# A state-space block with FFN on one core: the scan inside the chunks as a tree, in 13 steps

## The reference, cut to what matters

```python
s = sigmoid(silu(x @ s_w1.T + s_b1) @ s_w2.T + s_b2)
u = (x @ B_w.T + B_b) * s
def step(h, u_t):
    h = h @ A.T + u_t
    return (h, h)
_, hs = jax.lax.scan(step, h0, swapaxes(u, 0, 1))
y = hs @ C_w + C_b + x @ D_w.T + D_b
attn = y * sigmoid(x @ g_w.T + g_b)
x = x + layernorm(attn of layernorm(x))
x = x + layernorm(ffn of layernorm(x))      # square(relu(xf @ Ws1)) @ Ws2 + routed part
```

## Time and profile before

| what | value |
|---|---|
| median of 3 runs | 800.49 us (800.29 to 800.89) |
| the profiled execution | 800.6 us, of which the trace's span is 798.6 |
| PE busy | 783.3 us, 98% of the span |
| DVE, POOL, ACT busy | 605.9, 456.4 and 344.4 us |
| granted clock of PE | 0.998 of full speed |

### The profile page before, as it was taken

The page is one execution under the profiler, slowest core; times in us unless marked ns, Lnnn a source line. Parts: engine busy times, 40 slices in busy tenths (PEclk is TensorE's granted clock), DMA queues, the critical chain, the costliest instruction groups (busy, mean ns, idle before and its releaser), DMA issues. The chain is left out here.

```text
span 798.6 us, 10778 instructions
## 1 busy us (share of the span) xinstructions
PE 783.3 (98%) x3628; PEld 648.0 (81%) x3628; DVE 605.9 (76%) x1404; ACT 344.4 (43%) x554; POOL 456.4 (57%) x553
## 2 busy tenths in 40 slices
PE   7999999999999999999999999999999999999996
PEld 6878888888888888888888888888888888888875
DVE  7868896598956897678975889649896589734895
ACT  4535354344434554245443535435443444432353
POOL 1253658548465576466674665845757557644445
PEclk9999999999999999999999999999999999999999
DMA  8534434454355425552345533454425442232222
GB/s 269 207 107 158 137 94 138 160 184 134 87 177 174 161 89 158 183 187 80 95 143 185 185 101 96 147 185 168 149 80 182 150 143 80 78 133 87 65 113 106
DMA packets 40767, 110.90 MB, mean 139 GB/s; under 512 B 7044, under 2 KB 24836, under 8 KB 32903
## 3 DMA queue, kind: packets, MB, share of 16 engines
q1 hardware_dynamic: 40278, 110.00, 41.4%
q10 hardware_dynamic: 432, 0.20, 0.1%
HBM read 60.84 MB, written 33.61 MB: 118 GB/s over the span
## 5 line engine op out<-in xcount | busy, mean ns | idle before, releaser
L499 PE MATMUL TM<-gw_hi,xT_hi 128*128 128x512 f32 x256 | 107.3, 419 | 0.0
L1982 POOL TENSOR_TENSOR xres<-work,xres 128x512 f32<-128x512 f32 x56 | 75.1, 1341 | 52.8 <-DVE work L1332 52.8
L501 PE MATMUL TM<-gw_hi,xT_lo 128*128 128x512 f32 x256 | 100.6, 393 | 0.0
L501 PE MATMUL TM<-dw_hi,xT_lo 128*128 128x512 f32 x256 | 100.2, 391 | 0.0
L500 PE MATMUL TM<-gw_lo,xT_hi 128*128 128x512 f32 x256 | 100.0, 391 | 0.0
L499 PE MATMUL TM<-dw_hi,xT_hi 128*128 128x512 f32 x256 | 99.9, 390 | 0.0
L500 PE MATMUL TM<-dw_lo,xT_hi 128*128 128x512 f32 x256 | 99.6, 389 | 0.0
L996 ACT ACTIVATE work<-TM,nmz,rsz 128x512 f32<-128x512 f32 x62 | 48.2, 777 | 106.7 <-POOL nmz L1952 106.7
L1942 POOL TENSOR_TENSOR rsv<-rsv,negh 128x1 f32<-128x1 f32 x64 | 47.1, 736 | 82.3 <-DVE rsv L1328 82.2
L1997 POOL TENSOR_TENSOR x2T_lo<-work,x2T_hi 128x512 fp32r<-128x512 f32 x60 | 78.5, 1319 | 2.0 <-ACT x2T_hi L926 1.9
L1990 POOL TENSOR_TENSOR work<-work,xres 128x512 f32<-128x512 f32 x60 | 76.7, 1295 | 1.3 <-ACT work L996 1.3
(11 more groups left out here) (189 smaller groups left out, 2063.1 us busy)
## 6 DMA issues: line engine op xcount, KB each, us to landing
xres<-in_x SPq DMA_DIRECT2D x16, 1024.0 KB, 5.9
x_scratch<-xres SPq DMA_DIRECT2D x16, 1024.0 KB, 4.7
xin<-in_x SPq DMA_DIRECT2D x15, 1024.0 KB, 5.3
work<-x2q SPq DMA_DIRECT2D x120, 128.0 KB, 2.7
out<-work SPq DMA_DIRECT2D x30, 512.0 KB, 3.2
xin<-in_x_t SPq DMA_DIRECT2D x14, 1024.0 KB, 6.2
rows_in<-ln_scratch SPq DMA_DIRECT2D x14, 512.0 KB, 4.7
xin<-in_x SPq DMA_DIRECT2D x2, 512.0 KB, 5.0
```

The costliest lines, as they stand in the source:

```text
L499: eng.matmul(ps, lhs[0], rhs[0], start=first, stop=False)
L501: return eng.matmul(ps, lhs[1], rhs[0], start=False, stop=last)
L1982: eng.tensor_tensor(xres[:, j, :], work[:, j, :], xres[:, j, :], ALU.add).then_inc(S["x1_ok"], 1)
```

## The change

The part of the scan inside the chunks becomes a tree. Up: step 0 adds `A u_0, A u_2, A u_4, A u_6` to `u_1, u_3, u_5, u_7` (one product of 512 columns, one add of 512), step 1 adds `A^2 u_1, A^2 u_5` to `u_3, u_7` (256 columns), step 2 adds `A^4 u_3` to `u_7` and gives `carry`. Steps 3 to 9 are the doubling as before. Down: step 10 adds `A^4 carry` to `u_3`, step 11 adds `A^2` times `carry` and `u_3` to `u_1` and `u_5` (two products of 128), step 12 adds `A` times `carry`, `u_1`, `u_3`, `u_5` to `u_0`, `u_2`, `u_4`, `u_6` (products of 128 and 384 columns, one add of 512). Counted over a batch, 21 products become 15, with 2561 columns in both; 15 adds become 13, with 1793 columns before and 2561 after. The state of position 0 is ready only with step 12, for which `hs` of tile 0 now waits.

Four powers (A^3, A^5, A^6, A^7) are left out: 21 products and copies become 17. The orders of PE, DVE, ACT and POOL in the tails are written anew; in the startup DVE subtracts the first row of "b" earlier, and `low("d")` stands ahead of the second `u_of`. On POOL `z_rs` of tile 4 goes ahead of `ln1_rs`. The diff, cut to its core; DVE's lists of the tails are shown as order below:

```diff
-        POW = [1, 2, 3, 4, 5, 6, 7, 8, 16, 32, 64, 128, 256, 512]
+        POW = [1, 2, 4, 8, 16, 32, 64, 128, 256, 512]
...
-            POWERS += [(at[q], PA, at[q - 1]) for q in {1: (3,), 2: (5, 6, 7)}.get(k, ())]
-            if 3 * k in POW and k >= L:
-                POWERS.append((at[3 * k], plain, at[2 * k]))
...
                 if i == 0:
-                    for j in range(L - 1):
-                        m = eng.matmul(SC[:, 0:P], apt[:, idx[L - 1 - j], :], u[:, j, :],
-                                       start=(j == 0), stop=(j == L - 2))
-                elif i <= 7:
-                    s = 2 ** (i - 1)
+                    m = eng.matmul(SC[:, :], apt[:, idx[1], :], u[:, 0:7:2, :], start=True, stop=True)
+                elif i == 1:
+                    m = eng.matmul(SC[:, 0:2 * P], apt[:, idx[2], :], u[:, 1:6:4, :], start=True, stop=True)
+                elif i == 2:
+                    m = eng.matmul(SC[:, 0:P], apt[:, idx[4], :], u[:, 3, :], start=True, stop=True)
+                elif i <= 9:
+                    s = 2 ** (i - 3)
                     m = eng.matmul(SC[:, s:P], apt[:, idx[L * s], :], carry[:, 1:1 + P - s], start=True, stop=True)
+                elif i == 10:
+                    m = eng.matmul(SC[:, 0:P], apt[:, idx[4], :], carry[:, 0:P], start=True, stop=True)
+                elif i == 11:
+                    eng.matmul(SC[:, 0:P], apt[:, idx[2], :], carry[:, 0:P], start=True, stop=True)
+                    m = eng.matmul(SC[:, P:2 * P], apt[:, idx[2], :], u[:, 3, :], start=True, stop=True)
                 else:
-                    j = i - 8
-                    prev = carry[:, 0:P] if j == 0 else u[:, j - 1, :]
-                    m = eng.matmul(SC[:, 0:P], apt[:, 0, :], prev, start=True, stop=True)
+                    eng.matmul(SC[:, 0:P], apt[:, idx[1], :], carry[:, 0:P], start=True, stop=True)
+                    m = eng.matmul(SC[:, P:4 * P], apt[:, idx[1], :], u[:, 1:6:2, :], start=True, stop=True)
                 m.then_inc(S["scan_done"], 1)
...
                 scan_step(*a, 6)
                 G(*a, 2, {0: 7, 1: 8, 2: 9})
                 scan_step(*a, 10)
-                scan_step(*a, 11)
-                G(*a, 3, {1: 12})
-                scan_step(*a, 13)
-                scan_step(*a, 14)
+                G(*a, 3, {0: 11, 2: 12})
 
             def tail(b, rep):
                 a = (b, rep)
-                G(*a, 0, {0: 0, 1: 1, 2: 2})
+                G(*a, 0, {0: 0, 2: 1})
+                scan_step(*a, 2)
                 W1f(*a, 1, 0)
                 scan_step(*a, 3)
-                W1f(*a, 1, 1, {0: 4})
-                G(*a, 1, {0: 5, 1: 6})
-                scan_step(*a, 7)
-                G(*a, 2, {1: 8, 2: 9})
-                scan_step(*a, 10)
+                W1f(*a, 1, 1, {0: 4, 2: 5})
+                G(*a, 1, {0: 6, 1: 7})
+                scan_step(*a, 8)
+                G(*a, 2, {1: 9, 2: 10})
+                scan_step(*a, 11)
                 W2(*a, 4)
-                scan_step(*a, 11)
+                scan_step(*a, 12)
                 W2(*a, 5)
-                scan_step(*a, 12)
-                G(*a, 3, {2: 13})
+                G(*a, 3)
...
             def last_tail(b, rep):
                 a = (b, rep)
                 G(*a, 0, {2: 0})
-                scan_step(*a, 1)
-                W1f(*a, 1, 0, {1: 2, 2: 3})
-                scan_step(*a, 4)
-                W1f(*a, 1, 1, {0: 5, 1: 6})
-                scan_step(*a, 7)
-                G(*a, 1, {0: 8, 1: 9})
-                G(*a, 2, {1: 10, 2: 11})
+                W1f(*a, 1, 0, {0: 1, 2: 2})
+                scan_step(*a, 3)
+                W1f(*a, 1, 1, {0: 4, 1: 5, 2: 6})
+                G(*a, 1, {0: 7, 1: 8})
+                G(*a, 2, {0: 9, 1: 10})
...
             def hs(b, rep, j):
 
-                if j < L - 1:
-                    eng.wait_ge(S["scan_ok"], body_at("scan_ok", b, 8 + j))
+                if j == 0:
+                    eng.wait_ge(S["scan_ok"], body_at("scan_ok", b, 12))
...
             def scan_add(b, rep, i):
                 eng.wait_ge(S["scan_done"], body_at("scan_done", b, i))
-                if i == 0:
+                if i == 2:
 
                     if rep > 0:
                         eng.wait_ge(S["hs_hi_ok"], body_at("hs_hi_ok", b - 1, L - 1))
                     r = eng.tensor_tensor(carry[:, 1:P + 1], SC[:, 0:P], u[:, L - 1, :], ALU.add)
-                elif i <= 7:
-                    s = 2 ** (i - 1)
+                elif 3 <= i <= 9:
+                    s = 2 ** (i - 3)
                     r = eng.tensor_tensor(carry[:, 1 + s:P + 1], SC[:, s:P], carry[:, 1 + s:P + 1], ALU.add)
+                elif i == 10:
+                    r = eng.tensor_tensor(u[:, 3, :], SC[:, 0:P], u[:, 3, :], ALU.add)
                 else:
-                    j = i - 8
-                    r = eng.tensor_tensor(u[:, j, :], SC[:, 0:P], u[:, j, :], ALU.add)
+                    n, to = {0: (4, slice(1, 8, 2)), 1: (2, slice(3, 8, 4)), 11: (2, slice(1, 6, 4)),
+                             12: (4, slice(0, 7, 2))}[i]
+                    r = eng.tensor_tensor(u[:, to, :], SC[:, 0:n * P].rearrange("p (j n) -> p j n", n=P), u[:, to, :],
+                                          ALU.add)
                 r.then_inc(S["scan_ok"], 1)
...
+            ft_low(-1, -1, 0)
             ln1_norm(0, 1)
-            ft_low(-1, -1, 0)
             less_first_of("s1")
             ln1_norm(0, 2)
             ln1_norm(0, 3)
             l1_bn(0, 4)
+            less_first_of("b")
             l1_bn(0, 5)
...
             ft_low(-1, -1, 3)
-            less_first_of("b")
...
 
             def tail(b):
+                z_rs(b - 1, 4)
                 ln1_rs(b + 1, 0)
-                z_rs(b - 1, 4)
```

More of the change, by code:

```diff
@@ L814, in _ @@
             power(16)
-            power(17)
             H(-1, -1, 0, 0)
@@ L1016, in tail @@
                 zn(*a, 4)
+                hs(*a, 0)
                 zn(*a, 5)
+                gate(*a, 3)
                 hs(*a, 1)
-                gate(*a, 3)
                 zn(*a, 6)
@@ L1474, in first_tail, with tail @@
                 scan_add(*a, 0)
+                scan_add(*a, 1)
+                l1_bn(b + 1, 0)
+                scan_add(*a, 2)
+                l1_ag(b + 1, 0)
+                scan_add(*a, 3)
+                l1_bn(b + 1, 1)
+                scan_add(*a, 4)
+                l1_bn(b + 1, 2)
+                scan_add(*a, 5)
+                scan_add(*a, 6)
+                scan_add(*a, 7)
+                l1_bn(b + 1, 3)
+                scan_add(*a, 8)
+                l1_ag(b + 1, 1)
+                l1_ag(b + 1, 2)
+                l1_ag(b + 1, 3)
+                l1_bn(b + 1, 4)
+                l1_ep(b + 1, 0)
+                l1_bn(b + 1, 5)
+                scan_add(*a, 9)
+                scan_add(*a, 10)
+                scan_add(*a, 11)
+                l1_ag(b + 1, 4)
+                scan_add(*a, 12)
+                l1_ag(b + 1, 5)
+                l1_bn(b + 1, 6)
+                l1_bn(b + 1, 7)
+                l1_ag(b + 1, 6)
+                hs_low(*a, 0)
+                l1_ag(b + 1, 7)
+                hs_low(*a, 1)
+                l1_ep(b + 1, 1)
+            def tail(b, rep):
+                a = (b, rep)
+                scan_add(*a, 0)
                 l1_bn(b + 1, 0)
@@ L1487, in first_tail @@
                 scan_add(*a, 7)
+                l1_ag(b + 1, 2)
+                l1_ag(b + 1, 3)
+                l1_bn(b + 1, 6)
+                h2(*a, 1, 1)
                 scan_add(*a, 8)
                 scan_add(*a, 9)
-                hs_low(*a, 0)
-                l1_ag(b + 1, 2)
-                l1_ag(b + 1, 3)
+                l1_bn(b + 1, 7)
+                scan_add(*a, 10)
+                scan_add(*a, 11)
                 l1_ep(b + 1, 0)
-                scan_add(*a, 10)
-                l1_bn(b + 1, 4)
+                z_bn(*a, 4)
@@ L1861, in _ @@
             h1(-1, -1, 1, 1)
+            low("d")
             u_of(-1, -1, 1)
-            low("d")
             first_tail(0, 0)
```

118 lines of the change are left out of this document (33 added, 85 removed).

## The result

The changed kernel takes 802.91 us (median of 6 runs, 802.00 to 804.33) against 800.39 for the kernel before (800.18 to 800.89): ratio 1.0033, 95% interval 1.0022 to 1.0043. It is slower by 2.5 us, where 0.2 less was forecast, and just outside the range (802.8). Its profiled execution took 802.94 us with a span of 800.8.

What follows compares the result with a forecast made beforehand. PE was taken to bound every stage. Startup +0.4, first tail -0.7, six middle tails +0.1 and last tail -0.1 made -0.3 on the profiled 800.6 us; with the median 0.1 lower, 800.2 us, range 798.2 to 802.8.

Steps and rivals of the forecast that it cites:

- What bounds the kernel, and the price of a scan matmul: Whole kernel: PE bounds every stage; float32 products take two passes at two clocks a column, 0.87 us for 512 columns.
- the rival of one clock a column: All eight tails: a 512-column pass streams at one clock a column, 7.6 us less, 792.6; chance 6%.
- Steps that come too soon: Middle tails: new waits ahead of step 2 and step 9 offset the shorter work; six tails give +0.1 us.
- Step 2's 0.08: Middle tails: PE waits 0.08 us ahead of step 2, three products after the 256-column step 1.
- The 0.04 behind the second h2: Middle tails: add 8 stands behind the second h2 on DVE, so step 9 waits about 0.04 us.
- DVE's queue in the middle tails: Rival, six middle tails: add 8 comes 0.3 to 0.6 us late at step 9, 801.9 to 803.7; chance 18%.
- Startup: Before the first tail: subtraction for b delays the hidden layer, powers left out give 0.5 us back; net +0.4 us.
- The two powers: Startup, behind the first hidden layer: two of four omitted power products leave PE's queue, saving about 0.5 us.
- First tail: Batch 0's tail: two old waits go, step 10 waits 0.65 us and step 2 0.08; net -0.7 us.
- no two steps touch, so 1.3 us goes: First tail: products now stand between all steps, so the two waits at L543 vanish, -1.3 us.
- Last tail: Last batch's tail: h2 stands behind add 9, so no such wait, and less work gives -0.1 us.
- What else moves: POOL's later layernorm statistics, and hs of tile 0 on DVE: both stay hidden from PE, costed at nothing.

Runs made afterwards that it cites:

- e1: One of four follow-up kernels with the changed kernel's DVE startup order, first hidden layer at +0.43 to +0.59; which edit and time carry this label is not told.
- e4, e5, e7: Another of those four follow-up kernels, its startup clock held in the profile; which edit and time carry this label is not told.
- the four together: Changed kernel with DVE's old startup order (low part of d unmoved), first tail's step 12 later and add 9 earlier, last tail's step 1 ahead of FFN products: 801.28 us.

## Why the prediction was wrong

**What bounds the kernel, and the price of a scan matmul: right.** 512 columns cost 0.87, PE's busy time stayed (783.3 to 783.1 us), the first two middle tails fell by 0.10 and 0.04 us, and the rival of one clock a column (792.6) is refuted by every trace. The Trainium skill's four passes for a true float32 product ("FP8 and Floating Point Precision", section "TensorE Precision Notes") agree with the 0.87; its 518 cycles for 512 columns ("TensorE: Matmul & The Clock Gate", section "Back-to-back issue gap") do not hold for these products.

**Steps that come too soon: half right.** Step 2's 0.08 is there. The 0.04 behind the second h2 is not: add 8 starts at 143.96 and step 9 at 144.55, since DVE's instructions overlap more than the chain allowed. The six tails gave -0.36 in place of +0.1. So the rival with the right number (DVE's queue in the middle tails, 801.9 to 803.7) names the wrong place: nothing of the 2.5 us lies there.

**Startup: the forecast of the hidden layer came true by luck, and two things were left out.** The first hidden layer was forecast at +0.9 and came at +1.08, but about half of that is the clock's fall; in four profiles with the same order on DVE whose clock held there (in e1, e4, e5 and e7 of the record) it came at +0.43 to +0.59. The row of b that the sum took at 9.6 us had landed at 13.2, 8.7 us after its issue, and DVE subtracted at 13.50 without a wait. The two powers gave back 0.5 to 0.6, as forecast: the first gate at -0.04 and -0.09 in two such profiles, against +0.4.

What was left out first is the move of the low part of d ahead of the second u_of. The prediction put it at nothing, though the diff shows it and the earlier trace rows has the 0.7 us of u at L535. That is +0.7 at step 0. In the kernel after, u follows the low part of d at once:

```profile
39.86 2.93 DVE L204 TENSOR_TENSOR dw_lo<-xres,dw_hi 128x2048 fp32r<-128x2048 f32 x1 [0.59 <-ACT dw_hi L879]
42.72 0.74 DVE L1397 SCALAR_TENSOR_TENSOR u<-FM,b_col,sg 128x512 f32<-128x512 f32 x1
```

In the kernel before this instruction took 2.28 us; the difference of the two lengths, 0.65, is nearly all of the 0.7 (an estimate). Its old place, behind the second u_of, is not free either with the shorter step 0; a third place was not tried.

The second is the clock: the prediction took the granted clock of 1.00 as given. Both parts of the change to the startup went with more runs of a low mean (0.996 or less): DVE's new order with all 21 powers had 9 of 13, the powers left out with DVE's old order 9 of 22 (six of eleven in one kernel, three of eleven in that of the four together), both together 19 of 39 (the changed kernel and the three with edits of its tails), and neither of them 14 of 88 (the kernel before and the tree with the old startup). That PE's thinner work in the startup is the cause is not shown. These stretches had as little work of PE as those ahead of the falls, the first in the run with all 21 powers and DVE's order as changed, the second in that with step 12 moved:

```profile
10.00:12.00 2.00, 0.88 (x6) 0.69 (x6) 2.00 (x3) 0.36 (x3) 0.16 (x1) 1.00 0.99 363
```

```profile
8.00:10.00 2.00, 0.85 (x6) 0.69 (x6) 1.51 (x5) 0.94 (x3) 0.66 (x1) 1.00 0.94 298
```

In the first the clock held through the startup, in the second until 19 us. Filling the gaps did not settle it, and so what makes the clock fall stays open.

**First tail: the wrong step is "no two steps touch, so 1.3 us goes".** The two waits at L543 also covered ACT's read of two gates out of banks that the next products need. With step 12 three products before the end, the first Y waited 0.78 us, and when step 10's wait was taken away too, the last gate waited 0.47. From step 0 to the first Y it was +0.46 in place of -0.7; with step 12 moved, -0.41. That adds up: the two old places were worth 1.1 together and not 1.3 (at each a step and the next stood 0.77 apart, where two that do not wait stand 0.22 apart), and step 10, with ACT's read behind it, took back 0.7. The prediction followed the scan's chain and DVE's queue, and never asked which bank the next product writes.

**Last tail: the term -0.1 was +0.53.** The first FFN product came a step earlier than before and met POOL's x2T_lo; moving step 1 ahead of it took 0.41 away, together with a step 0 that came three products earlier.

**What else moves: right on the later statistics and on hs, and short of one wait.** The later statistics of POOL and hs of tile 0 show no wait of PE. But a wait for x2T_lo, behind a transfer, came up in bodies that were costed at nothing: +0.14 in batch 1 and +0.38 in the last body, where it is this row:

```profile
766.61 0.50 PE L496 MATMUL FM<-x2T_hi,f1w_hi 128*128 128x512 f32 x1 [0.57 <-POOL x2T_lo L1985]
```

Two other profiles with the same last tail have no such wait there; what makes it come was not separated.

**The range** ended at 802.8. Its upper end came from one rival, and it had no term for the clock, which alone is worth 0.5 to 2 us a run here. (Its lower end, 798.2, is 0.2 below what its own rival was worked out as.)

## What to carry to other kernels

A stall that a change removes may be the cover of another wait: before booking its gain, ask for each product behind it which bank it writes and who still reads that bank. A long instruction that is hidden behind a long step is laid bare when the step gets shorter, so price every neighbour of a shortened step. An instruction moved on one engine can get longer, or lengthen one of another engine, by what now runs beside it: read the lengths again after a move. And where the granted clock falls in some runs and not in others, compare its share of low runs before and after a change, and the clock of the same stretch, before trusting one profile: leaving out work that nobody needs may cost more than it saves, though here the cause of the falls was not shown.

## What the runs showed of the hardware that was not expected

The granted clock stood at its lower level for most of the 4 us from 12 to 16 in one execution; by their means, two of the six runs of the same kernel had no such fall. With only DVE's order changed it stood at 0.50 to 0.65 for 8 us in the profile, and five of six runs were low.

The low part of d, 2048 columns on DVE, took 2.28 us in the kernel before, 2.93 in the changed one and 3.31 with d behind u_of again. Beside it POOL ran low parts of its own, and in these profiles the one that began first kept its length while the other got longer. First the kernel before, where DVE began first, and POOL's instruction took 3.38 where the same one takes 1.27 or 1.28 in four other profiles; then the kernel after, where POOL began first (DVE's row stands above, at 39.86):

```profile
42.14 2.28 DVE L204 TENSOR_TENSOR dw_lo<-xres,dw_hi 128x2048 fp32r<-128x2048 f32 x1
42.20 3.38 POOL L204 TENSOR_TENSOR cw_lo<-work,cw_hi 128x512 fp32r<-128x512 f32 x1 [2.23 <-ACT cw_hi L885]
```

```profile
39.35 1.30 POOL L1991 TENSOR_TENSOR h_lo<-hf,h_hi 128x512 fp32r<-128x512 f32 x1 [0.59 <-DVE h_hi L1386]
```

The later one is longer by about the time in which the two overlap: 2.2 us before (it took 2.1 more), 0.8 after (0.65 more). In the run with the high part of d earlier, DVE began first again, and it was POOL's low part of h that took 3.24. With d behind u_of again POOL's cw_lo began first (42.13, 1.27 us), the low part of d took 3.31, and POOL's next low part, f1w_lo, begun at 43.36 beside it, took 4.42. No run was made to take the two apart.
